# Layer 1 attention of a two-layer gated network: score and maximum products on 32 array rows per head

## The reference

```python
q = (query @ Wq.T).reshape(B, T, 2 * H, D).transpose(0, 2, 1, 3)   # 32 score heads of D = 8
k = (query @ Wk.T).reshape(B, S, 2 * H, D).transpose(0, 2, 1, 3)
v = (query @ Wv.T).reshape(B, S, H, 2 * D).transpose(0, 2, 1, 3)   # 16 value heads of 16
attn = jnp.einsum('bhtd,bhsd->bhts', q * scaling, k)
attn = jax.nn.softmax(attn + causal, axis=-1)
attn = attn.reshape(B, H, 2, T, S)
attn = attn[:, :, 0] - lam * attn[:, :, 1]
out = jnp.einsum('bhts,bhsd->bhtd', attn, v)        # then RMS norm, gain, and Wo
# f: mixture of 8 experts (top 2) plus a shared one: silu(g) * u, then a down product
```

## Time and profile before

| | us |
|---|---|
| median of three runs | 2077.89 |
| the profiled execution | 2082.88 |
| its span on the core | 2081.2 |

### The profile page before, as it was taken

The page is one execution under the profiler, slowest core; times in us unless marked ns, Lnnn a source line. Parts: engine busy times, 40 slices in busy tenths (PEclk is TensorE's granted clock), DMA queues, the critical chain, the costliest instruction groups (busy, mean ns, idle before and its releaser), DMA issues.

```text
span 2081.2 us, 33061 instructions
## 1 busy us (share of the span) xinstructions
PE 1950.5 (94%) x11618; PEld 1431.0 (69%) x11618; DVE 1409.9 (68%) x3474; ACT 880.6 (42%) x1753; POOL 684.0 (33%) x846
## 2 busy tenths in 40 slices
PE   5888999999999999999999999999999999999998
PEld 3576676766767667686676766767676766767666
DVE  6856758577585775757766677666766577675783
ACT  3533624345252552525525255243643335343362
POOL 2533423243141441414414143132332333232341
PEclk8999999999999999999999999999999999999999
DMA  8736332262423524234242442415332163421630
GB/s 265 250 144 206 101 103 61 73 207 83 102 77 101 174 68 117 72 132 145 64 109 82 160 127 68 105 62 186 121 90 62 62 208 108 103 61 41 204 102 16
DMA packets 105261, 240.46 MB, mean 116 GB/s; under 512 B 16700, under 2 KB 26940, under 8 KB 104840
## 3 DMA queue, kind: packets, MB, share of 16 engines
q1 hardware_dynamic: 85080, 173.44, 27.8%
q0 software_dynamic: 14256, 43.94, 6.9%
q10 hardware_dynamic: 5760, 20.97, 3.0%
HBM read 179.67 MB, written 57.82 MB: 114 GB/s over the span
## 4 chain that ended last, share of the span: by engine, by line
PE 74%; DVE 12%; DMA 6%; issue 3%; ACT 1%; POOL 1%; DVEq 0%; ACTq 0%; POOLq 0%; SPq 0%
PE bank L452 21%; PE bank L616 15%; PE bank L535 11%; PE bank L501 10%; PE bank L551 7%; DMA qring<-mneg 4%; DVE bank L794 4%; DVE nmax L797 3%; PE bank L637 3%; PE bank L508 2%; PE bank L561 2%; PE bank L514 1%; DMA up_img<-xn 1%; DMA xnT<-mneg 1%; PE bank L463 1%
## 5 line engine op out<-in xcount | busy, mean ns | idle before, releaser
L452 PE MATMUL bank<-xnT,upring 128*128 128x512 f32 (+1 forms) x2208 | 710.3, 403 | 1.6 <-DVE hbuf L837 1.4
L794 DVE CUSTOM_DVE_ANT_0 bank<-bank,mask_strip 128x512 f32<-128x512 f32 (+1 forms) x768 | 478.9, 635 | 202.0 <-PE bank L501 200.1
L696 ACT ACTIVATE probs<-bank 128x512 f32<-128x512 f32 (+1 forms) x720 | 388.4, 556 | 289.2 <-PE bank L535 264.3
L452 PEld LDWEIGHTS bank<-xnT,upring 128*128 128x128 f32 x2208 | 402.9, 192 | 59.7 <-DVE hbuf L837 9.9
L501 PE MATMUL bank<-kring,qring 127*128 127x128 f32 (+3 forms) x1280 | 379.1, 350 | 22.4 <-DVE nmax L794 13.7
L535 PE MATMUL bank<-qring,kring 128*128 128x512 f32 (+1 forms) x880 | 356.9, 409 | 43.8 <-DMA qring<-mneg 22.5
L616 PE MATMUL bank<-wdown,hbuf 128*128 128x256 f32 x1408 | 324.4, 380 | 0.0
L501 PEld LDWEIGHTS bank<-kring,qring 127*128 127x128 f32 x1280 | 226.1, 193 | 114.3 <-DVE nmax L794 62.5
L616 PEld LDWEIGHTS bank<-wdown,hbuf 128*128 128x128 f32 x1408 | 263.4, 190 | 35.5 <-issue 1.7
L535 PEld LDWEIGHTS bank<-qring,kring 128*128 128x128 f32 x880 | 169.0, 193 | 130.6 <-issue 47.0
L1662 POOL TENSOR_SCALAR_AFFINE_SELECT probs<-probs 128x512 f32<-128x512 f32 x200 | 128.0, 640 | 375.7 <-ACT probs L696 375.2
(11 more groups left out here) (165 smaller groups left out, 2223.1 us busy)
## 6 DMA issues: line engine op xcount, KB each, us to landing
upring<-up_img SPq DMA_DIRECT2D x136, 512.0 KB, 3.9
upring<-up_img ACTq DMA_DIRECT2D x40, 512.0 KB, 5.3
q_img<-probs SPq DMA_DIRECT2D x32, 512.0 KB, 3.3
kring<-k_img SPq DMA_DIRECT2D x64, 256.0 KB, 2.9
qring<-q_img SPq DMA_DIRECT2D x32, 384.0 KB, 4.9
qring<-q_img SPq DMA_DIRECT2D x192, 64.0 KB, 2.0
q_img<-probs SPq DMA_DIRECT2D x32, 256.0 KB, 4.1
k_img<-probs SPq DMA_DIRECT2D x16, 512.0 KB, 5.7
```

Of the source, the lines that this page charges most:

```text
L452: last = nc.tensor.matmul(out_ap, part_a(a, pa, k), part_b(b, pb, k), start=(n == 0), stop=(n == len(steps) - 1))
L696: nc.scalar.activation(pr, pr if biased else scores, ACT.Exp, scale=scale).then_inc(s_exp, 1)
L794: nc.vector.tensor_tensor_reduce(scores, scores, mask_strip[:, T - w:T], 1.0, -BIG, ALU.add, ALU.max, nmax[:, u % 2, g0, qt:qt + 1]).then_ ...
```

## The change

- **Rings.** For layer 1, q has the same layout as k: four heads on 32 partitions each, three places for q and three for k, without zero rows. The maximum row of each head is row 31 of its 32. The code that zeroed rings (four ScalarE copies at the start, a GpSimd memset of `xnT[0]` and one of a part of `kring[0]` per batch) goes, with its waits. Loading q is one DMA instead of four.
- **Products.** A score or maximum product of layer 1 reads only the 32 rows of its head. Score pack i and maximum pack i stand next to each other in TensorE's order and use different groups of 32 rows (heads 2, 3, 0, 1 against 0, 1, 2, 3).
- **Packs.** A layer-1 unit has 12 packs: 4 of 512 columns, 4 of 384, and 4 of 256 + 128 for one head each. In these last four the score side takes two products and two exponentials, the maximum side two products and two masked VectorE instructions. The bf16 mask products and the TENSOR_REDUCE instructions of layer 1 go.
- **Up products.** They stand in groups of three after packs 2, 5 and 8, in the front in groups of 4, 5, 4 and 5 after packs 2, 5, 8 and 11; in unit 11 in groups of three after packs 1 and 4.

```diff
+PACKS_OF = (PACKS, 12)
+PACKS_TO_1 = (4, 8, 12, 12)
+SCORE_PACKS_1 = [(kts, g) for kts in ((0,), (1,), (2, 3)) for g in (2, 3, 0, 1)]
+MAX_PACKS_1 = [(qts, g) for qts in ((3,), (2,), (1, 0)) for g in range(4)]
+R1 = 32
+UP_GROUPS = {2: 0, 5: 1, 8: 2}
...
-                for g in range(G4):
-                    sp.dma_start(q_of(u)[32 * g:32 * g + 32, g, :].bitcast(F32), q_img[1][4 * w + g]).then_inc(done, 16)
-                sp.dma_start(k_of(u).bitcast(F32),
-                             k_img[1][4 * w:4 * w + 4].rearrange("g r n -> (g r) n")).then_inc(done, 16)
+                for ring, img in ((q_of(u), q_img), (k_of(u), k_img)):
+                    sp.dma_start(ring.bitcast(F32), img[1][4 * w:4 * w + 4].rearrange("g r n -> (g r) n")).then_inc(done, 16)
...
+            if l == 1:
+                qts, g = MAX_PACKS_1[i]
+                rows = slice(R1 * g, R1 * g + R1)
+                c = 0
+                for qt in qts:
+                    w = P * (qt + 1)
+                    last = nc.tensor.matmul(bk[:, c:c + w], q_of(u)[rows, qt * P:(qt + 1) * P], k_of(u)[rows, 0:w],
+                                            start=True, stop=True)
+                    c += w
+                last.then_inc(s_mp[k], 1)
+                return
...
+            if l == 1:
+                kts, g = SCORE_PACKS_1[i]
+                rows = slice(R1 * g, R1 * g + R1)
+                c = 0
+                for kt in kts:
+                    w = T - P * kt
+                    last = nc.tensor.matmul(SC[n % 2][:, c:c + w], k_of(u)[rows, kt * P:(kt + 1) * P],
+                                            q_of(u)[rows, kt * P:T], start=True, stop=True)
+                    c += w
+                last.then_inc(s_sc, 1)
+                return
...
+            if layer_of(u) == 1:
+                qts, g = MAX_PACKS_1[i]
+                c = 0
+                for qt in qts:
+                    last = masked(c, qt, g)
+                    c += P * (qt + 1)
+                last.then_inc(s_mr[k], 1)
+                return
...
-                        if not lower and more and i < UP_INSIDE:
-                            pe_up(pe, tile, i // UP_STEPS, i % UP_STEPS, 1)
+                        if not lower and more and i in UP_GROUPS:
+                            n = UP_GROUPS[i]
+                            pe_up(pe, tile, n // 2, 3 * (n % 2), 3)
...
-                for i in range(PACKS):
+                for i in range(packs_of(UNITS[0])):
                     pe_max_pack(pe, UNITS[0], i)
-                    if i:
-                        pe_up_between(pe, FRONT_TILES[3], i - 1, 3, PACKS - 1)
+                    if i % 3 == 2:
+                        pe_up_between(pe, FRONT_TILES[3], i // 3, 3, 4)
```

More of the change, by code:

```diff
@@ L91, in q_slot, with packs_of, packs_ahead, max_packs_ahead @@
     return (0, 1, 1, 0)[u] if u < UNITS[0] else (u - UNITS[0]) % 3
+def packs_of(u):
+    return PACKS_OF[layer_of(u)]
+def packs_ahead(u):
+    return sum(packs_of(i) for i in range(u))
+def max_packs_ahead(u):
+    return packs_ahead(u) - PACKS if u else 0
 def q_rows(u):
@@ L272, in gated_layers_kernel @@
         turns = (1, U_ALL - 1)
[L273 removed]
+        packs = (PACKS, max_packs_ahead(U_ALL))
         s_mp, s_mr, s_mT = two("max_scores_in_psum", packs), two("max_reduced", packs), two("max_transposed", turns)
@@ L277, in gated_layers_kernel @@
         s_ring[UNITS[0] - 1] = sem("ring_of_last_unit_loaded", 32)
[L278 to L283, removed]
+        s_ring1 = [sem(f"ring_in_place_{i}_loaded", 32 * len(range(i, UNITS[1], 3))) for i in range(3)]
+        s_sc = sem("scores_in_psum", packs_ahead(U_ALL))
+        s_exp = sem("exps_ready", packs_ahead(U_ALL))
         s_es0 = sem("first_distance_factors_ready", 1)
@@ L679, in act_exps @@
         def act_exps(act, u, i):
-            n = PACKS * u + i
+            n = packs_ahead(u) + i
+            if layer_of(u) == 1:
+                kts, g = SCORE_PACKS_1[i]
+                act.wait_ge(s_sc, so_far(s_sc, n + 1))
+                c = 0
+                for kt in kts:
+                    w = T - P * kt
+                    wait_place(act, u, kt)
+                    if u == U0[1] and i == 0:
+                        wait_images(act, 1, 4)
+                    last = nc.scalar.activation(probs_of(u, kt)[:, g, :], SC[n % 2][:, c:c + w], ACT.Exp, scale=EXP_SCALE[1])
+                    c += w
+                last.then_inc(s_exp, 1)
+                return
             kt, g0, heads = SCORE_PACKS[i]
@@ L1196, in sp_batch @@
                     if u == 1:
-                        if b:
-                            sp.wait_ge(s_kz, before(s_kz, 1))
                         ring_load(sp, UNITS[0] - 1)
@@ L1247, in unit @@
                         wait_ring(pe, u + 1)
-                    for i in range(PACKS):
+                    for i in range(packs_of(u)):
                         pe_score_pack(pe, u, i)
@@ L1663, in pool_batch @@
                                                 channel_multiplier=-1).then_inc(s_pm, 1)
-                        if u == U_ALL - 2 and kt == 1 and more_batches:
-                            pool.wait_ge(s_sc, so_far(s_sc, PACKS * u))
-                            nc.gpsimd.memset(kring[0][0:MROW, UNITS[0] - 1, :].bitcast(F32), 0.0).then_inc(s_kz, 1)
                         if u == UNITS[0] and kt < 2:
```

87 lines of the change are left out of this document (41 added, 46 removed).

## The result

The changed kernel takes 2459.3 us (median of 4 runs, 2451.4 to 2468.3), the kernel before 2078.1: 1.1825 times as long, interval 1.1795 to 1.1856. The forecast was 2154, the range ended at 2225. The direction was right, the size was not: 381 us more, where 76 had been reckoned.

A forecast was written before the change was run, and what follows sets the result against it. VectorE was taken to set the pace in layer 1's packs, where TensorE is also at its limit. 2082.9 + 56 (units) + 16 (front) + 4 (unit 11) = 2158.9, as a median 2154 us; range 2085 to 2225.

The forecast's parts named there:

- the rival on the clock: TensorE, waiting in every unit's packs, drops to 1.2 GHz there: 2215 to 2275 us, 2245 standing for it; chance 0.12.
- The unit, +1.0: Each of 56 layer-1 units with maxima: VectorE's walk 1.27 us longer, 0.27 back by an earlier start; 56 us in all.
- The switch, valued 0: Changing between 32-row and 128-row products on TensorE was given no cost in the sum; 34 us left to the upper end.
- Side by side: A pair's score and maximum product start together on separate row groups, so VectorE starts 0.50 us after, instead of 0.77.
- That rival (0.15, 2209): A pair's score and maximum product run one after the other: 0.99 us more a unit, 2209 us; chance 0.15.
- The front, +2.0: Layer 1's stretch before unit 4, eight times: VectorE's maxima end later, +2.0 us each, bounds 1.0 and 2.7; 16 us.
- Unit 11, +0.5: Unit 11, eight times: one more pack and four more exponentials, +0.5 us each, bounds 0 and 1.0; 4 us.
- What goes, 0: Dropping the ScalarE copies, a GpSimd memset and ring loads saves nothing, at most 3.9 us for the copies.
- The tail, "stays 3.01": Unit's end, from transpose of the maxima to next score product: unchanged at 3.01 us.
- No gaps: Rival: VectorE never waits for maximum products after the groups of up products and runs at its floor: 2092 us; chance 0.13.
- faster: Rival: narrow maxima cost 0.58 us a pack, not 0.74, and no gap appears: about 2055 us; chance 0.10.
- the one for its being wrong: Sign against the forecast: unit under 11.5 us, maxima not paced by VectorE, or matmuls 0.4 us or more apart at lower clock.

The follow-up runs named there:

- the first experiment: Changed kernel with layer-1 products back on 127 and 128 rows, from rings with zeros, packs and groups kept: 2173.9 us, 1.0467 times the kernel before.
- the third: Changed kernel with score pack i and maximum pack i on the same group of 32 rows: 2487.0 us, 1.1963 times the kernel before.
- the fourth experiment: Changed kernel with up products standing singly between the pairs instead of in groups, 32 rows kept: 2418.0 us, 1.1615 times the kernel before.

## Why the prediction was wrong

**The step that failed** is the weighing of the rival on the clock: 0.12 and 2245 us, with "Against it: a group of up products comes every 2 to 3 us, where that stretch had one." Both halves were wrong.

- *Its trigger.* I took TensorE's waits in the packs as the cause, from a stretch with seven products in 3.5 us, and the frequent groups as the cure. The first experiment has those packs and groups and keeps 0.986; the third has them too and falls to 0.844. The fourth falls to 0.856, and in its unit TensorE was busy for all of the stretch ahead of the fall, while the kernel with added products holds full clock with 9.88 of 12.40 busy. What sets the low clock off here is products on 32 rows. The Trainium skill (TensorE: Matmul & The Clock Gate, HAM oscillation) also ties a lost clock to long idle gaps between matmuls. The earlier trace rows fit idle time as a cause, but the fourth experiment has none and loses the clock all the same; the measurement decides.
- *Its size.* "A 0.24 becomes 0.48" was charged to nine up products, 2.2 us at most. The low clock reaches into everything that follows, while the sum kept every product at 0.24 and the tail at 3.01. The tail alone grew from 3.01 to 4.77. A unit in the batch takes 120.0 / 7 = 17.15 against 13.19 in the first experiment; less 0.36 for the rows at full clock that is 3.6 us for the clock, 56 x 3.6 = 202 us (an estimate). Another 21.4 - 15.95 = 5.5 us lie in each front, 44 us in eight, and 2.2 in each unit 11, 17 us. With the 20 of the 0.36 it makes 283 of the 285. The parts of the front and of unit 11 were not split: they hold the switches between 32 and 128 rows as well as the clock.

Then the other terms, each against the first experiment, where the clock doesn't hide them.

- *The unit, +1.0.* Right in mechanism and near in size for packs and groups on 128 rows; for the changed kernel at full clock it would be 1.26 + 0.36 = 1.6, an estimate. The seven units of a batch take 92.3 us there, 13.19 each, +1.26 for a forecast +1.0; the walk without the side by side start, 1.27, is what this kernel ought to show. Behind it two errors cancel: narrow packs start 0.60 apart, not 0.74, where the next one is there in time (833.21 to 833.81 above), and the gaps are 0.40 to 0.43, not 0.18 to 0.31.
- *The switch, valued 0.* From the last maximum product to the first up product is 0.42 in the changed kernel (825.12 to 825.54) and 0.34 with 128 rows (1014.27 to 1014.61); from there to the next pair 0.89 and 0.69. That is 0.28 for two switches, 0.14 each, above the 0.1 that I took as the nearest row. In the fourth experiment, whose up products stand singly, a pair and an up product take 0.85 (838.06 to 838.91); at 0.24 for the pair side by side and 0.24 for the up product that leaves 0.37, 0.19 a switch. Both are estimates. The Trainium skill (TensorEngine Tiling (Array Packing), Key Properties) says that a change of mode drains TensorE. The trace agrees as far as each change costs time.
- *Side by side.* Right: 823.74 and 823.75. VectorE starts 0.56 after the pair's first product, forecast 0.50, and 0.75 in the first experiment, where the pair runs in turn. That rival (0.15, 2209) is out.
- *The front, +2.0.* The first experiment has 15.95 for 14.5, +1.45: in the bounds, and 4 us too much in the sum.
- *Unit 11, +0.5.* It was +1.87 (13.74 for 11.87), above the bound of 1.0, and 11 us too little in the sum. Which of its waits makes that was not traced.
- *What goes, 0.* Nothing in the measurements contradicts it; it wasn't tried by itself.
- *The tail, "stays 3.01".* At full clock it does, 2.93.

The three terms together were 76 us, and 96 were measured. "No gaps" and "faster" are out as well: gaps stand at packs 3, 6 and 9 in both timelines, and not even the twelve packs alone, at 2097.1, come under the kernel before. Packs, groups and their waits thus account for 96 of the 381 us, the 32 rows for 285, by the estimate above nearly all by way of the clock. Of the signs that the prediction named, the one for its being wrong came true: in the slow stretch the up products of a group stand (832.45 - 830.87) / 3 = 0.53 apart at a granted clock of 0.50.

Open stays what the chip goes by in 32-row products. Zeros in the other rows are enough to keep the clock, as the first experiment shows, so it is not the useful arithmetic. Whether the overlap of such products plays a part beside their rows stays open too: no kernel ran 32-row products strictly one after another.

## What to carry to other kernels

A product on 32 rows streams as many columns as one on 128, and it can halve the clock of all that stands around it, as it did here in packs with 32 such products to 12 full ones: read the granted clock of the stretch before counting the columns saved. If a stage is bound by VectorE, freeing TensorE there gives nothing, and grouping its fillers opens gaps in VectorE's feed that single ones don't. Price a fall of the clock over all that runs until it is back, not over the products that were moved.

## What the runs showed of the hardware

- The same products in the same packs and groups, with 96 of 128 rows zero, keep TensorE at a mean clock of 0.986; addressed as 32 rows they leave it at 0.839, or 0.844 with score and maximum product on the same rows.
- With products on 32 rows the granted clock fell from 1.00 to 0.50 although TensorE was busy without a pause before it, 6.20 of 6.20 us in the stretch shown (fourth experiment).
- Adding 504 full-row products that nobody reads took 104 us off, and the mean clock rose from 0.839 to 0.956.
- Four products, each on its own group of 32 rows (two pairs), start within 0.01 us; a change between 32 and 128 rows costs 0.14 to 0.19 us, by estimate.
- A masked maximum on VectorE takes 0.44 us for 256 columns and 0.33 for 128, start to start 0.35 to 0.38 and 0.25.
